# The two copies of the value product move from ScalarE to VectorE in a fused cross-attention and mixture-of-experts kernel

## The reference

```python
y_dca, y_main = y[:, -DCA:, :], y[:, :-DCA, :]                      # DCA = 16
kv_dca = (y_dca @ Wkv_dca + bkv_dca).reshape(b, DCA, 2, H, HD)      # H = 16 heads of HD = 32
q = _ln((x @ Wq + bq).reshape(b, s1, H, HD), qn_w, qn_b)            # x: layernormed rows
kv = concat([y_main @ Wk + bk, y_main @ Wv + bv]).reshape(b, s2, H, 2 * HD)
k, v = _ln(kv[..., :HD], kn_w, kn_b), kv[..., HD:]
ctx = _attn(q, k, v) + _attn(q, k_dca, v_dca)                       # softmax attention per head
x = x + ctx @ Wo + bo
x = x + moe(_layernorm(x))       # 6 experts, the best 2 per batch element, exact gelu
```

## Time and profile before

| | |
|---|---|
| median of 3 runs | 1198.97 us (1198.28 to 1206.18) |
| the profiled execution | 1200.36 us, its span 1198.6 us |
| busy over the span | PE 965.9 us, DVE 813.2 us, ACT 636.2 us, POOL 294.4 us |
| steps b = 1 to 13, one after the other | 594.57 us for 13, 45.11 to 47.11 us each |

### The profile page before, as it was taken

The page is one execution under the profiler, slowest core; times in us unless marked ns, Lnnn a source line. Parts: engine busy times, 40 slices in busy tenths (PEclk is TensorE's granted clock), DMA queues, the critical chain, the costliest instruction groups (busy, mean ns, idle before and its releaser), DMA issues. The chain is left out here.

```text
span 1198.6 us, 17317 instructions
## 1 busy us (share of the span) xinstructions
PE 965.9 (81%) x5020; PEld 647.9 (54%) x5020; DVE 813.2 (68%) x1706; ACT 636.2 (53%) x1658; POOL 294.4 (25%) x203
## 2 busy tenths in 40 slices
PE   1867888888888889789788888556379999999998
PEld 0334444445445445445445445323368888888886
DVE  5446767768768677777777776451877776777774
ACT  0227677677677677776776776653532221313131
POOL 0482523513514514404404314000100000000000
PEclk9886999999999899999999999677689999999999
DMA  7132534534624624615625515466111111111100
GB/s 245 35 88 72 135 91 116 135 81 115 143 72 115 150 56 116 153 59 126 143 65 131 137 52 109 119 210 213 71 36 53 52 52 52 52 52 52 52 35 36
DMA packets 56405, 116.31 MB, mean 97 GB/s; under 512 B 13944, under 2 KB 22392, under 8 KB 56120
## 3 DMA queue, kind: packets, MB, share of 16 engines
q1 hardware_dynamic: 53760, 115.16, 35.4%
q10 hardware_dynamic: 2616, 0.79, 0.3%
HBM read 47.24 MB, written 17.30 MB: 54 GB/s over the span
## 5 line engine op out<-in xcount | busy, mean ns | idle before, releaser
L452 POOL TENSOR_TENSOR vs<-vs,neg_half 128x16 f32<-128x16 f32 x66 | 199.9, 3058 | 465.1 <-DVE vs L882 464.6
L762 ACT ACTIVATE sc<-sc,nm 128x240 f32<-128x240 f32 x512 | 225.0, 456 | 98.9 <-DVE ed L930 98.9
L925 DVE TENSOR_REDUCE pm<-sc 128x64 f32<-128x1024 f32 x128 | 156.1, 1219 | 33.0 <-PE sc L601 31.8
L771 ACT ACTIVATE pt<-sc 128x1024 f32<-128x1024 f32 x128 | 125.3, 1021 | 83.3 <-PE sc L622 83.3
L1345 ACT ACTIVATE hb<-hb 128x352 f32<-128x352 f32 x64 | 30.8, 498 | 248.1 <-DVE hb L1435 248.0
L554 PE MATMUL ring<-wq,xT 128*128 128x512 f32 x256 | 137.2, 686 | 15.2 <-ACT xT L730 15.1
L601 PE MATMUL sc<-KS,QS 96*128 96x256 f32 x512 | 105.1, 336 | 46.8 <-ACT sc L762 42.5
L601 PEld LDWEIGHTS sc<-KS,QS 96*128 96x128 f32 x512 | 75.1, 202 | 86.9 <-ACT sc L762 61.5
L567 PE MATMUL ring<-wkv,cT 128*128 128x512 f32 (+1 forms) x256 | 121.2, 608 | 0.0
L646 PE MATMUL ring<-wo,ot 128*128 128x512 f32 x256 | 116.7, 599 | 0.6 <-DVE ot L972 0.6
L762 ACT ACTIVATION_READ_ACCUMULATOR sc<-sc,nm 128x1 f32 x512 | 117.2, 229 | 0.0
(11 more groups left out here) (137 smaller groups left out, 1650.6 us busy)
## 6 DMA issues: line engine op xcount, KB each, us to landing
QS<-q_hi SPq DMA_DIRECT2D x128, 128.0 KB, 3.0
KS<-k_hi SPq DMA_DIRECT2D x128, 128.0 KB, 3.0
xin<-in_x_dram SPq DMA_DIRECT2D x16, 512.0 KB, 3.7
QS<-q_lo SPq DMA_DIRECT2D x64, 128.0 KB, 2.9
KS<-k_lo SPq DMA_DIRECT2D x64, 128.0 KB, 2.9
xres<-in_x_dram SPq DMA_DIRECT2D x16, 512.0 KB, 3.4
x_scratch<-xres SPq DMA_DIRECT2D x16, 512.0 KB, 2.7
x<-x_scratch SPq DMA_DIRECT2D x16, 512.0 KB, 3.3
```

What stands on the lines that cost most here:

```text
L452: pool.tensor_tensor(w, w, neg_half[0:rows, :], ALU.pow).then_inc(rstd, 1)
L762: last = act.activation(s, s, ACT.Exp, bias=nm[:, t, h:h + 1], accum_out=den[:, t, h:h + 1])
L771: act.activation(pt[g % 2][:, (p % 2) * 2:(p % 2) * 2 + 2, :], sc[p % 2][:, :, :], ACT.Exp).then_inc(sc_evac[p % 2], 1)
L925: dve.tensor_reduce(pieces, s.rearrange("p h (c n) -> p h c n", n=DCA), AX_X, ALU.max, negate=True).then_inc(g_max, 1)
```

## The change

The two copies of `V0` and `V1` leave ScalarE's program, where they stood between exponentials 0 and exponentials 1, and come into VectorE's, behind the maxima 0 and 1 and ahead of the two key normalisations. They read the same banks, write the same buffer and free the banks through the same semaphores. There are 16 pairs of them: in step `p2` and in the steps b = 0 to 14. No matmul and no DMA is added, removed or moved.

```diff
@@ ScalarE, body
             if attn:
                 exps(b, 0)
-            if keyed:
-                for c in range(NC):
-                    copy_out(step, b, f"V{c}", v[1 - par][0:ROWS[c], c:c + 1, :], D)
             if attn:
                 exps(b, 1)
                 exps(b, 2)
@@ VectorE, body
                 group_max(b, 0)
                 group_max(b, 1)
             if keyed:
+                for c in range(NC):
+                    bank = wait_full(dve, step, f"V{c}", b)
+                    dve.tensor_copy(v[1 - par][0:ROWS[c], c, :], bank[0:ROWS[c], 0:D]
+                                    ).then_inc(taken(step, f"V{c}"), 1)
                 for k in range(T, T + NC):
                     normalise(k, norms(b + 1) + k, head_norm_values(k))
             if attn:
```

## The result

The changed kernel takes 1206.22 us (median of 7 runs, 1205.05 to 1213.07) against 1200.54 us (median of 7, 1198.28 to 1206.18): a ratio of 1.006 with a 95% interval of 1.0039 to 1.0082, that is 4.7 to 9.8 us. The forecast was 1205.6 us, 0.55% slower. The profiled execution of the changed kernel is the slowest of its seven, 1213.07 us with a span of 1211.3 us, so single steps must be read from it and not the total.

A forecast was written before the change was run, and what follows sets the result against it. Bound by a chain of waits through maxima, exponentials, scores and WO0, with VectorE and ScalarE equally loaded. 4.1 + 0.4 + 2.1 = 6.6 us on 1198.97 gave 1205.6 us, 0.55% slower; range 1199.5 to 1213.

The forecast's parts named there:

- the sum: Whole kernel: 4.1 us in full steps, 0.4 in b = 0 and 2.1 in p2, 6.6 us slower; chance 0.62.
- SP's queue: In p2, query DMAs go out until 86.8, key DMAs want to start at 87.3 and find it free: no cost.
- The price of a copy: Each V copy on VectorE: 0.61 us at the slow PSUM pace, taken from the upper bound.
- rival A: V copies on VectorE run at double pace, 0.35 us each: +2.6 us, 1201.6 us; chance 0.13.
- ScalarE's relief: 0.96 us per step taken off ScalarE is worth 0, since it waits 1.98 us ahead of exponentials 2 and 3.
- Rival D: ScalarE's relief reaches the end through exponentials 3 to 7: 10.9 us faster, 1188.1 us; chance 0.03.
- Maximum 2 and scores 4: In full steps maximum 2 moves behind the copies, delaying exponentials 2; scores 4 are 0.20 to 0.43 us late.
- WO1 and all behind it: WO1 follows scores 4 at once and the rest of the step follows: no slack, 4.07 us in 14 full steps.
- Step b = 0: No WO0, so no slack for VectorE: exponentials 3 at 106.49 against 106.12, 0.4 us late.
- Step p2: Start-up: normalisations wait for V1 and its copy, so key transposes come at 75.97, 2.1 us late.
- B: TensorE's clock falls less often; with no falls 13 steps take 8.1 us less, 1197.5 us; chance 0.08.
- C: TensorE's clock falls more often: up to 17.9 us more, 1223.5 us; chance 0.14 with at least a third of that.

The follow-up runs named there:

- e1: Changed kernel with the V copies on VectorE only in steps b = 0 to 14, on ScalarE in p2: 1205.3 us, 1.0046 against the kernel before.
- e2: Changed kernel with the V copies on VectorE only in p2, on ScalarE in steps b = 0 to 14: 1203.1 us, 1.0022 against the kernel before.
- e3: Kernel before with both V copies on VectorE, in steps behind maximum 2, in p2 behind normalisations and query splitting: 1200.3 us, ratio 1.0006.
- e9: Kernel before with only the affine copies of KT0 and KT1 moved to VectorE, behind maximum 4, nothing reordered: 1197.9 us, ratio 0.9987.
- e4: Changed kernel with each V copy made twice, the extra one into a buffer nobody reads: 1223.1 us, 1.0202 against the kernel before.
- e7: Kernel before with only the V0 copy moved to VectorE, ahead of the normalisations; V1 stays on ScalarE: 1201.5 us, ratio 1.0023.
- e5: Changed kernel with the queries of p2 split ahead of the V copies on VectorE: 1207.6 us, 1.0079 against the kernel before.
- e6: Changed kernel with the V copies behind the two key normalisations, in the steps and p2: 1202.2 us, 1.0033 against the kernel before.
- e10: Kernel before with new orders alone (WO1 split around XT0, scores 5, XT1; XT copies earlier; residual addition later), affine copies on ScalarE: 1205.8 us, ratio 1.0053.
- e11: The change made on a reordered kernel (new orders, affine copies on VectorE): 1190.1 us, 0.9922 against the kernel before.

## Why the prediction was right

The forecast of 0.55% is measured as 0.6% (0.39 to 0.82), and the halves, 0.46% (e1) and 0.22% (e2), add up to 0.68%. The mechanism is the one forecast. That the number came so near is in part luck: two terms that the sum took at nothing, SP's queue and the clock, add to the profiled execution, whose own pieces (3.4 in the start-up, 0.4 and 6.4 in the steps) make 10.2 us where the sum had 6.6, and the median over the executions came out lower than that. The start of the V product in p2, ahead of the change, alone varies from 65.6 to 71.5 us over the 13 profiles, so the total of one execution says little. Step by step:

- **The price of a copy.** All copies take 678 to 692 ns, and behind the V1 copy the next instruction starts after 0.60 or 0.61 us in every one of the 16 pairs. From the V0 copy to the V1 copy it is 0.60 to 0.88 us in the full steps, since V1 may not be ready. The upper bound was right and rival A, 0.35 us, is refuted.
- **ScalarE's relief is worth nothing.** Its idle time ahead of exponentials 2 and 3 went from 1.98 to 1.76 + 1.08 us (the prediction said 1.9 and 1.1). e3 keeps the relief and takes away the push: 1.0006. Rival D is refuted; e9 says the same of 1.3 us.
- **Maximum 2 and scores 4.** 331.85 for 331.89, 335.42 for 335.46.
- **WO1 and all behind it.** WO1 starts late in its step in 13 of the 14 full steps by 0.18 to 0.45 us, and in b = 3 early by 0.13; together 3.7 us, where the working gave 4.07. The difference is mostly b = 3, where the kernel before was late for a reason of its own. The 13 steps take 46.21 us in the mean, a little over the 46.0 given as a sign of being right. Twice the work (e4) costs 20.1 us in the steps, half of it (e7) nothing: the slack is what decides, and the change lies just past it.
- **Step b = 0.** Exponentials 2 and the logarithm: from scores 0 to the logarithm 25.58 instead of 25.15 us, 0.43 for 0.4.
- **Step p2.** The key transposes come 2.2 us late, for 2.1. But the term of SP's queue, taken at nothing ("so they still find the queue free"), was mis-sized: scores 0 come 2.7 us late in e2 and 3.4 in the changed kernel, so the term is 0.6 to 1.2 us. The working had the last query DMA out at 86.8 and the key DMAs wanting to start at 87.3, a margin of 0.5 us. One of the last query DMAs took 1.56 us in e2 and 2.04 in the changed kernel to issue, instead of 0.59, and the margin was gone. e5, with the query DMAs out early, has 27.37 instead of 28.72 us, 2.0 over the kernel before and no more; e6, with the key transposes on time, still has scores 0 2.9 us late.
- **The clock, rivals B and C.** B is refuted: none of the changed kernel, e1, e5 and e6 has fewer steps at 0.93 than the kernel before. A small part of C is there, which the sum took at nothing. The profiled executions of the changed kernel, e1 and e5 have 6.4 to 6.9 us more in the 15 steps than the kernel before, of which WO1's lateness makes 3.7 (5.3 in e1), with two or three steps at 0.93 where all five kernels without the lateness have one. That is 1 to 3 us, three times out of three, and not the third of C's price (6 us) that the chances asked for. Why the falls come more often, and why they do not in e4, no run shows. The totals are too wide to tell (their interval of 4.7 to 9.8 us holds the terms above without the clock, 6.9 to 7.5 us, and the same with 1 or 2 us for it).

## What to carry to other kernels

Work that goes to another engine is free where it fits into a measured wait of that engine, behind the point that others wait for, and dear ahead of that point: the same two copies cost 0.6% ahead of maximum 2, 0.06% and no measurable difference behind it, and four times as much when doubled. The engine that is relieved gives nothing back if it waits later anyway (1.98 us here); it paid only when the order around that wait was changed in the same step (e9 and e10 nothing or worse, both 0.9%). And where an instruction that releases DMAs moves, count the issues that then stand in front of the next user of their queue: a margin of 0.5 us behind twelve issues of 0.59 us each was none, as soon as one of them took longer.

## What the runs showed of the hardware

**A DMA issue of SP that takes three times as long.** SP's issues of one DMA take 0.59 us; in p2 single ones took 2.04 us (changed, from 87.20), 1.56 (e2, from 84.95), 1.67 (e6, from 79.40) and 1.88 (e7, from 82.88). In each of the four, two things start within 0.6 us of it: VectorE's cast `k_hi` (87.62, 85.33, 79.34, 82.95) and GpSimd's power of the variances (87.77, 85.47, 79.49, 83.10). In the kernel before, SP had nothing to issue at that point. But neither of the two is needed: in e10 an issue of p2 took 1.73 us while VectorE stood idle and GpSimd was in a memset (SP's queue, then GpSimd):

```profile
76.12 1.73 SPq L384 DMA_DIRECT2D QS<-q_lo  x1
...
75.85 3.29 POOL L446 MEMSET KS<- 2x3840 f32 x1
```

In e11 one took 1.13 us at 78.59, again with VectorE idle, and in e4 one beside the same cast and power took only 0.84. In the full steps before, the longest of 56 `q_lo` and of 112 `k_hi` issues take 1.73 and 2.17 us, with medians of 0.59. Of the six kernels whose query DMAs go out late, four have one of over 1.5 us among them, and of the seven others one has. What brings it about no run here tells.

**A cast that ends 0.55 us after the memset beside it.** The cast `q_hi` of 128x1024 from SBUF to SBUF takes 0.69 us in its plain form (`k_hi` in the earlier trace rows), but in p2, beside GpSimd's memsets of `KS`, it took 2.06 us (before), 2.00 (changed), 1.58 (e4), 3.38 (e6) and 3.62 (e7). GpSimd and VectorE of before, then of e7:

```profile
66.61 3.30 POOL L446 MEMSET KS<- 4x3840 f32 x1
...
68.40 2.06 DVE L954 CAST q_hi<-qf 128x1024 fp32r<-128x1024 f32 x1
```

```profile
73.28 3.29 POOL L446 MEMSET KS<- 4x3840 f32 x1
...
73.50 3.62 DVE L954 CAST q_hi<-qf 128x1024 fp32r<-128x1024 f32 x1
```

The memset ends at 69.91 and 76.57, the cast at 70.46 and 77.12: 0.55 us later in both, and in all 13 profiles. So the cast takes as long as the memset in progress has left, and 0.55 us. The next memset takes 3.73 us instead of 3.29. The plain copy out of PSUM shows nothing of the kind in the same stretch: 0.69 us in e7. The Trainium skill, SBUF — State Buffer, section "SBUF: two separate sides", says that VectorE in its two-port mode and GpSimd share a pair of ports and lock each other out; the trace agrees, with these numbers.
